# Audio tower layer: second chunk's token chain among the first chunk's projections, norms at other places of the second scan

## The reference

```python
h = patches @ tok_W.T + tok_b                       # 512 features
h = h + block(layernorm(h))                         # mamba and MLP, below
h = h + down(silu(gate(n)) * up(n)),  n = layernorm(h)

# block(x):
zxbcdt = rmsnorm(x, rms1_w) @ in_proj_w.T           # z 1024, x 256, B 256, C 1024, dt 128
dt = softplus(dt_in @ dt_proj_w.T + dt_proj_b)
state = exp(dt * A) * state + (dt * x) * B          # 1024 channels x 16 states, along a token axis
y = (sum over 16 states of C * state + D_skip * x) * silu(z)
h1 = x0 + y @ out_proj_w.T
out = h1 + (silu(hn @ gate_w.T) * (hn @ up_w.T)) @ down_w.T,  hn = rmsnorm(h1, rms2_w)
```

## Time and profile before

| | |
|---|---|
| median of 3 runs | 675.78 us (672.87 to 676.73) |
| the profiled execution: time / span | 675.06 us / 673.3 us |
| busy: PE, PEld, DVE, ACT, POOL | 631.5, 505.7, 418.0, 346.4, 429.2 us |
| mean granted TensorE clock | 0.98 |
| chunk 0's units begin / chunk 1's begin (DVE) | 36.58 us / 204.25 us |
| chunk 0's `out` begins / its first MLP begins (PE) | 218.64 us / 245.81 us |

### The profile page before, as it was taken

The page is one execution under the profiler, slowest core; times in us unless marked ns, Lnnn a source line. Parts: engine busy times, 40 slices in busy tenths (PEclk is TensorE's granted clock), DMA queues, the critical chain, the costliest instruction groups (busy, mean ns, idle before and its releaser), DMA issues.

```text
span 673.3 us, 8617 instructions
## 1 busy us (share of the span) xinstructions
PE 631.5 (94%) x2846; PEld 505.7 (75%) x2846; DVE 418.0 (62%) x532; ACT 346.4 (51%) x773; POOL 429.2 (64%) x244
## 2 busy tenths in 40 slices
PE   4969998799999989999979999999999999999998
PEld 3736765466665757777747777766999998999998
DVE  4077896889887879889887888851322223332132
ACT  4359889358989364434356433422542442653441
POOL 0176785437786999987877987644455463445461
PEclk9879998799999989999989999999999999999999
DMA  8699997489999969988866898533443453134421
GB/s 340 238 365 364 318 299 268 141 258 357 350 373 348 390 250 349 413 336 318 320 247 257 320 330 323 191 125 122 138 149 126 125 157 126 63 130 132 146 67 44
DMA packets 49164, 163.50 MB, mean 243 GB/s; under 512 B 4320, under 2 KB 18528, under 8 KB 48480
## 3 DMA queue, kind: packets, MB, share of 16 engines
q1 hardware_dynamic: 49120, 162.95, 68.9%
HBM read 145.24 MB, written 17.69 MB: 242 GB/s over the span
## 4 chain that ended last, share of the span: by engine, by line
PE 75%; DVE 11%; ACT 5%; POOL 3%; issue 3%; DMA 2%; SPq 0%; DVEq 0%; ACTq 0%; POOLq 0%
PE work L992 54%; PE da L992 15%; DVE da L784 6%; PE work L1002 5%; DVE hs L794 3%; POOL hs L447 2%; ACT L522 2%; ACT da L548 1%; DMA bb<-b_rows 1%; DMA c_rows<-c_rows 1%; DMA sm<-small 0%; POOL hs L460 0%; DVE a L849 0%; ACT z L665 0%; DVE work L809 0%
## 5 line engine op out<-in xcount | busy, mean ns | idle before, releaser
L784 DVE TENSOR_TENSOR_SCAN da<-da,hs 128x580 f32<-128x580 f32 (+1 forms) x128 | 191.1, 1493 | 39.6 <-POOL hs L447 22.2
L447 POOL TENSOR_TENSOR hs<-dtx,bb 128x1160 f32<-128x1160 f32 (+1 forms) x64 | 171.2, 2677 | 61.1 <-PE work L1002 54.1
L426 POOL TENSOR_TENSOR ws<-wraw,ws 128x1024 fp32r<-128x1024 f32 x40 | 101.4, 2536 | 92.8 <-ACT ws L557 92.8
L992 PE MATMUL work<-sq,wraw 128*128 128x290 f32 x512 | 125.7, 406 | 1.1 <-DVE sq L882 1.1
L992 PE MATMUL work<-hn,win 128*128 128x290 f32 (+1 forms) x336 | 104.4, 459 | 16.6 <-DVE hn L857 8.1
L992 PEld LDWEIGHTS work<-sq,wraw 128*128 128x128 f32 x512 | 96.5, 189 | 30.0 <-issue 1.6
L548 ACT ACTIVATE da<-dt,a_neg 128x261 f32<-128x261 f32 (+1 forms) x256 | 118.2, 493 | 0.0
L794 DVE TENSOR_TENSOR hs<-da,cb 128x580 f32<-128x580 f32 (+1 forms) x128 | 105.2, 822 | 10.7 <-DMA cb<-c_rows 2.7
L992 PEld LDWEIGHTS work<-hn,win 128*128 128x128 f32 x336 | 65.5, 200 | 50.7 <-issue 26.0
L545 ACT COPY da<-zeros 128x58 f32<-128x58 f32 (+1 forms) x128 | 27.6, 216 | 126.0 <-DVE hs L794 125.8
L557 ACT CAST ws<-wraw 128x1024 fp32r<-128x1024 f32 x48 | 50.3, 1048 | 70.2 <-PE da L992 34.4
(11 more groups left out here) (98 smaller groups left out, 655.2 us busy)
## 6 DMA issues: line engine op xcount, KB each, us to landing
wraw<-w_stream SPq DMA_DIRECT2D x104, 512.0 KB, 4.1
bb<-b_rows SPq DMA_DIRECT2D x32, 700.0 KB, 7.1
cb<-c_rows SPq DMA_DIRECT2D x32, 700.0 KB, 5.6
bb<-b_rows SPq DMA_DIRECT2D x32, 580.0 KB, 8.0
cb<-c_rows SPq DMA_DIRECT2D x32, 580.0 KB, 6.0
c_rows<-c_rows SPq DMA_DIRECT2D x8, 875.0 KB, 10.8
c_rows<-c_rows SPq DMA_DIRECT2D x8, 725.0 KB, 6.6
win<-w_in SPq DMA_DIRECT2D x4, 1024.0 KB, 13.4
```

The lines of the kernel that those rows point to most:

```text
L426: nc.gpsimd.tensor_tensor(ws[:, k % NW, 1, :], wraw[:, split_loads[k] % NRAW, :], ws[:, k % NW, 0, :].bitcast(F32), ALU.subtract).then_inc ...
L447: nc.gpsimd.tensor_tensor(hs[:, u % NH, 0:NQ * n].rearrange("p (n t) -> p n t", t=n), dtx[:, t % 2, 0:n].unsqueeze(1).to_broadcast([P, NQ, ...
L784: nc.vector.tensor_tensor_scan(da[:, j, 0:w], da[:, j, 0:w], hs[:, u % NH, j * w:(j + 1) * w], 0.0, ALU.mult, ALU.add).then_inc(scan_done, 1)
L992: last = nc.tensor.matmul(dst, w, x, start=(k == 0), stop=(k == len(pairs) - 1))
```

## The change

`tokc` becomes four steps `tok` of one product each, and chunk 1's stand in slots 5, 6, 8 and 9, `mean` in slot 10, `ln1` in 11 and `rms1` in 13, each first in its slot, ahead of chunk 0's projections there. `in_dt`, `in_b` and `in_x` stand in slots 14 to 16, tiles 0 to 5 of chunk 1 in 17 to 28, slot 29 is empty, tile 6's `dtp`, `xs` and `in_z` stand in 30 and 31. Slot 32 is empty. Beside the norms of the second scan stand `in_c` of tile 6 and `in_z` of tile 7 (`rms2`), `dtp` of tile 7 (`ln2_mean`) and `in_c` of tile 7 (`ln2_var`). `tok`, `mean` and `ln1` join `LATE`. Chunk 1's squares go to `th` and `acc`, its reciprocal roots to `rstd` and `rstd_ln`, so that `mean`'s bank is free after L842 and `ln1`'s after L846. ACT does the squares of `rms2` in the slot before it, the root first in its slot, and both for `ln2_var` in the slot of `ln2_mean`. On DVE `PLACE` puts the last two `out` and `rms2` after the first half of their unit, `ln2_mean` after the first scan, `ln2_var` ahead of it. Chunk 0's `gate_y` for tiles 0 to 6 stands in the middle of the unit of quarter 2, not at the end of that of quarter 1.

```diff
+def tokens(c):
+    return [("tok", c, k) for k in range(KD)]
...
-    bg += [[("dtp", 0, 7), ("in_c", 0, 7)], [("xs", 0, 7), ("in_z", 0, 7)]]
-    bg += [[("tokc", 1)], [("mean", 1), ("ln1", 1)], [("rms1", 1)], [("in_dt", 1), ("in_b", 1, 0)],
-           [("in_x", 1, 0), ("in_b", 1, 1)], [("in_x", 1, 1)]]
+    bg += [[("in_c", 0, 7), ("in_z", 0, 7)], [("dtp", 0, 7), ("xs", 0, 7)]]
+
+
+    for u, s in zip((5, 6, 8, 9, 10, 11, 13), tokens(1) + [("mean", 1), ("ln1", 1), ("rms1", 1)]):
+        bg[u].insert(0, s)
+    bg += [[("in_dt", 1), ("in_b", 1, 0)], [("in_x", 1, 0), ("in_b", 1, 1)], [("in_x", 1, 1)]]
     bg += two_tiles(1, 0) + two_tiles(1, 2) + two_tiles(1, 4)
+    bg += [[], [("dtp", 1, 6)], [("xs", 1, 6), ("in_z", 1, 6)]]
     assert len(bg) == UNITS
     slots += list(enumerate(bg))
     o = outs(0)
-    first = [[("dtp", 1, 6), ("in_c", 1, 6), ("xs", 1, 6)], [("xs", 1, 7)], o[0:2], o[2:4]]
+    first = [[], [("xs", 1, 7)], o[0:2], o[2:4]]
     rest, left = [], UNITS - len(first)
     for s in m_steps(0):
 
-        rest += {"rms2": [("in_c", 1, 7), s, ("in_z", 1, 6)], "ln2_mean": [s, ("in_z", 1, 7)],
-                 "ln2_var": [s, ("dtp", 1, 7)]}.get(s[0], [s])
+        rest += {"rms2": [("in_c", 1, 6), s, ("in_z", 1, 7)], "ln2_mean": [s, ("dtp", 1, 7)],
+                 "ln2_var": [s, ("in_c", 1, 7)]}.get(s[0], [s])
...
-LATE = ("dtp", "xs", "in_c", "in_z", "out")
-SEAM = (("in_c", 1, 7), ("in_z", 1, 6), ("in_z", 1, 7), ("dtp", 1, 7))
+LATE = ("dtp", "xs", "in_c", "in_z", "out", "tok", "mean", "ln1")
+SEAM = (("in_c", 1, 6), ("in_z", 1, 7), ("dtp", 1, 7), ("in_c", 1, 7))
+
+PLACE = {("out", 0, 2): 2, ("out", 0, 3): 2, ("rms2", 0): 2, ("ln2_mean", 0): 1, ("ln2_var", 0): 0}
...
-                if kind == "tokc":
-                    if c == 0:
+                if kind == "tok":
+                    k = s[2]
+                    if (c, k) == (0, 0):
                         act.wait_ge(tokb_done, 1)
-                    else:
-                        full(act, ("xs", c - 1, KI - 1))
-                        act.wait_ge(b_stored, 16 * 2 * c)
-                    for k in range(KD):
-                        name = ("tokc", c, k)
-                        full(act, name)
-                        nc.scalar.activation(a(c, k), bank(name), ACT.Identity, bias=tok_bc[:, k:k + 1]).then_inc(centered, 1)
-                        nc.scalar.activation(sq[:, k, 0:n], bank(name), ACT.Square,
-                                             bias=tok_bc[:, k:k + 1]).then_inc(free_of(name), 1)
+                    full(act, s)
+                    nc.scalar.activation(a(c, k), bank(s), ACT.Identity, bias=tok_bc[:, k:k + 1]).then_inc(centered, 1)
+                    nc.scalar.activation(token_square(c, k), bank(s), ACT.Square,
+                                         bias=tok_bc[:, k:k + 1]).then_inc(free_of(s), 1)
...
-                    if v >= 1:
-                        act.wait_ge(norm_done, KD * v)
                     full(act, s)
                     link(nc.scalar.activation(ln, bank(s), ACT.Ln, bias=eps_ap))
                     nc.scalar.activation(inv, ln, ACT.Exp, scale=-1.0).then_inc(inverse_done, 1)
-                    act.wait_ge(h_done, KD * (c + 1))
-                    nc.scalar.activation(bank(("mean", c)), ln, ACT.Exp, scale=-0.5).then_inc(rstd_done, 1)
+                    if c == 0:
+                        act.wait_ge(h_done, KD * (c + 1))
+                        nc.scalar.activation(bank(("mean", c)), ln, ACT.Exp, scale=-0.5).then_inc(rstd_done, 1)
+                    else:
+                        nc.scalar.activation(ln, ln, ACT.Exp, scale=-0.5).then_inc(rstd_done, 1)
...
+                    if c >= 1 and kind == "in_x":
+                        full(act, ("xs", c - 1, KI - 1))
+                    if c >= 1 and kind == "in_b":
+                        act.wait_ge(b_stored, 16 * 2 * c)
+                    if c >= 1 and kind == "in_dt":
+                        full(act, ("dtp", c - 1, KI - 1))
...
-                    norm = [s for s in steps if s[0] in ("rms2", "ln2_var")]
-                    if norm:
-
-                        n = steps.index(norm[0])
-                        between = [steps[n - 1]] if steps[n - 1] == SEAM[2] else []
-                        first = steps[:n - len(between)] + [("squares",) + norm[0]]
-                        second = between + [("root",) + norm[0]] + steps[n + 1:]
+
+                    if i + 1 < len(slots) and ("rms2", 0) in slots[i + 1][1]:
+                        second.insert(0, ("squares", "rms2", 0))
+                    if ("rms2", 0) in steps:
+                        first, second = [("root", "rms2", 0)], [s for s in steps if s[0] != "rms2"]
+                    if ("ln2_mean", 0) in steps:
+                        first = [("squares", "ln2_var", 0), ("root", "ln2_var", 0)]
+                        second = [s for s in steps if s[0] != "ln2_mean"]
+                    if ("ln2_var", 0) in steps:
+                        first, second = [], [s for s in steps if s[0] != "ln2_var"]
...
-                    if unit % QU == 1 and unit > QU:
+
+                    if unit < UNITS and unit % QU == 2 and unit > QU:
+                        parts.insert(2, ("gate", unit // QU - 1))
+                    if unit > UNITS and unit % QU == 1:
                         parts.append(("gate", unit // QU - 1))
...
+                    for s in reversed([s for s in others if s in PLACE]):
+                        parts.insert(PLACE[s], s)
+                    others = [s for s in others if s not in PLACE]
```

More of the change, by code:

```diff
@@ L104, in schedule @@
 def schedule():
-    slots = [(None, [("bmean", 0), ("tokc", 0), ("mean", 0), ("ln1", 0), ("rms1", 0), ("in_dt", 0), ("in_b", 0, 0), ("in_b", 0, 1),
+    slots = [(None, [("bmean", 0), *tokens(0), ("mean", 0), ("ln1", 0), ("rms1", 0), ("in_dt", 0), ("in_b", 0, 0), ("in_b", 0, 1),
                      ("dtp", 0, 0), ("in_c", 0, 0), ("in_x", 0, 0), ("xs", 0, 0)]),
@@ L163, in work_bank_uses @@
                 ring = RINGS[2]
-            names = {"tokc": [("tokc", s[1], k) for k in range(KD)], "rms1": [],
-                     "gu": [(s, "gate"), (s, "up")]}.get(s[0], [s])
+            names = {"rms1": [], "gu": [(s, "gate"), (s, "up")]}.get(s[0], [s])
             for n in names:
@@ L615, in step @@
                     nc.scalar.activation(inv, ln, ACT.Exp, scale=-1.0).then_inc(inverse_done, 1)
[L616 to L617 removed]
+                    if c == 0:
+                        act.wait_ge(h_done, KD * (c + 1))
+                        nc.scalar.activation(bank(("mean", c)), ln, ACT.Exp, scale=-0.5).then_inc(rstd_done, 1)
+                    else:
+                        nc.scalar.activation(ln, ln, ACT.Exp, scale=-0.5).then_inc(rstd_done, 1)
                 elif kind == "rms1":
[L619 removed]
+                    var = bank(("ln1", c)) if c == 0 else rstd[:, 0:n]
                     log_tables()
                     act.wait_ge(scaled_var, c + 1)
[L622 to L623 removed]
+                    link(nc.scalar.activation(rstd[:, 0:n], var, ACT.Ln, bias=eps_ap))
+                    nc.scalar.activation(var, rstd[:, 0:n], ACT.Exp, scale=-0.5).then_inc(rstd_done, 1)
                 elif kind in ("rms2", "ln2_var"):
@@ L706, in step @@
                             gated_high(i)
-            for unit, steps in late(slots, 1):
+            for i, (unit, steps) in enumerate(late(slots, 1)):
                 if unit == 0:
@@ L857, in step @@
                         nc.vector.scalar_tensor_tensor(out=hn[:, k, 0:n], in0=a(c, k), scalar=small_ap(S_W1, k),
-                                                       in1=bank(var), op0=ALU.mult, op1=ALU.mult).then_inc(norm_done, 1)
+                                                       in1=bank(var) if c == 0 else rstd[:, 0:n],
+                                                       op0=ALU.mult, op1=ALU.mult).then_inc(norm_done, 1)
                     dve.wait_ge(norm_done, KD * (v + 1))
-                    dve.sem_inc(free_of(var), 1)
-                    dve.sem_inc(free_of(("mean", c)), 1)
+                    if c == 0:
+                        dve.sem_inc(free_of(var), 1)
+                        dve.sem_inc(free_of(("mean", c)), 1)
                 elif kind == "rms2":
@@ L1041, in step @@
                     product(s, [(mean_w[:, :], sm[:, S_TOKB:S_TOKB + KD])], KD)
-                elif kind == "tokc":
+                elif kind == "tok":
                     pe.wait_ge(pat_loaded, 16 * (c + 1))
                     pe.wait_ge(tokw_done, 1)
-                    for k in range(KD):
-                        product(("tokc", c, k), [(tokw[:, k * P:(k + 1) * P], pat[:, OFF[c]:OFF[c] + n])])
+                    product(s, [(tokw[:, s[2] * P:(s[2] + 1) * P], pat[:, OFF[c]:OFF[c] + n])])
                 elif kind == "mean":
@@ L1049, in step @@
                 elif kind == "ln1":
-                    product(s, [(mean_w[:, :], sq[:, k, 0:n], free_of(("tokc", c, k)), uses[("tokc", c, k)][1] + 1)
```

(1 more changed line is left out.)

20 lines of the change are left out of this document (14 added, 6 removed).

## The result

The changed kernel takes 680.37 us (median of 5 runs, 678.68 to 681.46) against 675.78: 1.0069 times the kernel before, interval 1.0044 to 1.0095. It is slower, where 669 was forecast and faster held most of the chance. Its profiled execution took 678.68 us, with a span of 676.9.

The account below looks back on a forecast made before the run. The prediction took PE, busy 94%, to set the pace, with DVE close behind. It summed +3.0 (scan's end and `out`), -4.5 (`rms2`) and -4.4 (`ln2`) to -5.9 from 675.06, so 669.2, forecast as 669.0; range 658 to 674.

Parts of the forecast that it names:

- the wait for C rows: Near unit 30 of chunk 0's scan: DVE's wait behind six weight loads, 0 to 2.65 us, taken as 1.0.
- PE's gain of 4.0 by ss26: Up to the end of unit 26's state sum on PE: 11.4 us of old losses gone, less 7.4 of new ones.
- what the MLPs give back: Second scan: 2.5 us lost to a bank wait in the MLP behind `ln2`; none counted behind `rms2`.
- the three seams: PE's idle gaps between the chunks, at `rms2` and at `ln2`, with lower clock behind: some 26 us in all.
- The chain among the units: Chunk 0's units: new PE waits of 1.6 (`ln1`), 1.6 (`rms1`), 2.4 and 1.0 us (state sums), plus 0.8 of clock.
- The end of the scan: End of chunk 0's scan: DVE's line of 23.0 us behind ss26 leaves `y_done` of tile 7 unchanged; `out` ends 3.0 later.
- Rival 2: Slots 5 to 11: ACT is overrun, each slot loses a table load's length, 9.0 us more, time 678.2; chance 0.09.
- rival 3: Both MLP starts: DVE, not PE, sets them, half of the norms' 8.9 us returns as bank waits, 673.6; chance 0.15.
- The clock: At `out`: PE's clock falls in 6.5 us of idle time ahead of it, costing 2.0 us (0 to 3.4).
- `rms2`: Chunk 0, end of `out` to first MLP: 6.8 us instead of 11.3, gain 4.5 (0 to 4.5).
- `ln2`: Chunk 0, `ln2_mean` to second MLP: PE starts 6.9 us earlier, 2.5 lost to a bank wait, gain 4.4 (1 to 6.9).
- The gates: Chunk 0's gates in mid-unit: free where PE trails DVE, else state sums wait 2.4 (unit 12) and 1.0 us (unit 16).

Follow-up runs that it names:

- both mended: Changed kernel with the root of the second chunk's first norm kept in PSUM and the six weight loads issued over six slots: 674.40 us, 0.9982.
- The part by itself: Kernel before with only the second scan's steps beside the norms, DVE places and ACT order, tile 6's `in_z` in slot 32: 670.63 us, 0.9922.

## Why the prediction was wrong

**The steps that failed.** The prediction had the chain's move with the end of the scan and `out` at +3.0 us, and expected the norms to outweigh it. In the traces it is +10.0 (from unit 5 to the end of `out`, 186.1 against 176.0). The largest failed term is the wait for C rows, taken as 1.0 and measured as 4.2. The second is PE's gain of 4.0 by ss26, which was 1.6, with an operand's move put at nothing that cost 1.3. The third is what the MLPs give back: nothing and 2.5 were forecast, 1.3 and 4.4 measured.

**What bounds the kernel.** Behind the second term stands a reading that failed too. From PE's 94% and its full windows the prediction took it that PE's gaps between the chunks were PE's to win back. With the chain moved they are not, up to `out(0)`: giving PE 11.9 us of free time instead of 8.1 brought nothing, and DVE's line with its hand-overs to ACT and POOL set the pace. For the kernel before this is argued and not shown, since no run took PE's gaps away and left the chain in place, and DVE waits 6.1 us for PE there. The prediction had half of this, where it said that DVE's pace cannot rise behind ss26. It let DVE's line ahead of ss26 follow PE's, and put PE's 4.0 us of gain into it. On DVE unit 20 came 4.6 us later than before (92.45 us behind unit 5 against 87.84).

**The chain among the units, "PE gains 4.0".** PE gained 9.1 - 7.5 = 1.6 by ss26. Two waits were foreseen well (1.27 for 1.6 at `ln1`, 1.02 for 1.0 at unit 16), but `in_dt` waited 4.05 for 1.6, 1.44 came that was not foreseen, and the lower clock cost 2.2 at `in_dt` (4.60 for 2.36) and not 0.8. That is 10.0 where 7.4 were forecast. Of the miss of 2.4, 1.3 is L876's (139.49 - 138.18): the prediction counted the move of the roots from PSUM to SBUF ("same instructions as before") at nothing. The other 1.3 is still there with both mended (138.37 against 137.05), and `rms1`'s operand may have up to 0.7 of it. The prediction's 26 us for the three seams do not come out of its rows either: 11.4, 2.97 + 1.8 and 4.96 + 1.10 + 1.8 make 24 (1.8 is what a variance at the lower clock takes longer). No later term rests on it.

**The end of the scan.** "DVE has, in line, ... 23.0" was right but for 0.9: 23.94 and 23.93 once the loads don't disturb it. The C-row wait was the mis-sized term, 1.0 in a range of 0 to 2.65, and measured 4.2 (28.1 against 23.9 with the loads spread). The range's upper end came from a row where the wait stands in unit 33. Moved to units 30 and 31, the waits delay the gate behind them and with it unit 28's state sum. The row of before was no price for this: where it stood, spreading the loads gave nothing.

**Rival 2**, slower at 678.2 with `out` beginning after 223, comes near the number (680.37 and 225.65) by chance, since its mechanism is not what happened: seven slots were to lose a table load's length each, and PE waited only twice there, 0.56 and 1.27, the second time for a bank that DVE frees. What did grow is DVE's waiting for ACT between units 5 and 20, from 7.3 to 12.6 us. The rule that the prediction sets beside rival 3 is that of the Trainium skill ("Trainium Kernel Development and Optimization", Best Practices): weight loads' busy share, and not matmul's, tells how near PE is to its limit. The prediction set it aside since the gaps' releasers seemed to speak against the slack. Up to `out(0)` it would have been the better guide, as far as the kernels with the chain moved show. Behind that, 5.9 of the 11.7 us won at the norms came through, in a kernel where the share is 75% all the same.

**The clock** took 2.5 for 2.0 in `out`, inside the stated 0 to 3.4. Not foreseen was a further stretch at the lower clock, 363.8 to 367.2, behind the bank wait of the second MLP.

**`rms2`**: 4.8 for 4.5, right, but the first MLP gave 1.3 back, 1.10 of it in a bank wait for which the prediction had nothing. **`ln2`**: PE begins 6.9 earlier, exactly as worked out, with 0.83 open for the squares (0.8). The bank wait was 2.04 for 2.5; with the smaller ones behind it and the clock, 4.4 are given back in all, so that 2.5 of gain are left and not 4.4. Rival 3 had "half of the 8.9" come back as bank waits; here 5.8 of 11.7 did. The part by itself still gains 0.8% (0.9922).

**The gates** were costed at 3.4 us in two waits. One came, 1.02, and the gates alone gain 0.3%.

What stays open: that DVE's hand-overs with ACT and POOL make unit 20 late, with 2.3 us more idle time than before, was read from the list of waits and is not settled by a run. A version of the chain which spares DVE these waits was not tried, and neither was one with both roots back in PSUM.

## What to carry to other kernels

An idle gap of the busiest engine is a gain only if the next event that all engines wait for comes earlier by closing it. Before moving a chain, follow the line of the engine that the meeting point waits for (here DVE to `y_done`), add the chain's hand-overs to it at the new place, and see if it arrives sooner. Price each change of an operand's place as an instruction of its own, and look up what POOL does beside it at that time. And let each part of a compound change run alone: here a gain of 1.3% was hidden under a loss of 2.0%.

## What the runs showed of the hardware

**A DVE multiply with both operands in SBUF, beside a POOL instruction.** Single ones of L876 took 2.35, 1.11, 1.01 and 1.01 us. With one operand in PSUM they took 0.51 each, although POOL was busy beside most of them too. The timelines of DVE and POOL, first before, then after:

```profile
121.82 1.79 DVE L849 TENSOR_TENSOR a<-a,work 128x350 f32<-128x350 f32 x4
122.27 2.44 POOL L447 TENSOR_TENSOR hs<-dtx,bb 128x1160 f32<-128x1160 f32 x1 [1.88 <-PE work L1002]
```
```profile
101.06 2.45 POOL L461 TENSOR_TENSOR hs<-dtx,bb 128x1160 f32<-128x1160 f32 x1 [6.01 <-PE work L1038]
...
103.48 1.08 POOL L496 TENSOR_TENSOR pair<-sp_w,pair 128x290 f32<-128x290 f32 x1
104.63 0.86 POOL L498 TENSOR_TENSOR pair<-pair 128x290 f32<-128x290 f32 x1
105.57 0.86 POOL L500 TENSOR_TENSOR dt<-dt,pair 128x290 f32<-128x290 f32 x1
```

The first one ends at 103.90, 0.4 behind POOL's 103.51, as if it had run only then; the others alternate with POOL's, which grow too (1.08, 0.86, 0.86 for 0.80, 0.70, 0.70 with the root in PSUM). L885, both operands in SBUF with POOL idle, takes 2.06 for four, and 2.76 in the run where it meets one of POOL. The Trainium skill ("SBUF — State Buffer", SBUF: two separate sides) has this rule: a DVE instruction with two SBUF inputs and a GpSimd instruction that reads SBUF exclude each other for their whole length. The trace agrees, with the 2.35 and the alternation behind it. The prediction overlooked it.

**Queued loads.** Behind six weight loads issued within 2.90 us, C rows on the same queue took 14.87 us from issue to landing, and a later issue took 5.70, where the others there take 0.3 to 1.2. With one load a slot the changed kernel's issues there take 0.32 to 0.69.

**Clock.** Behind 4.99 to 5.99 us of idle time ahead of `out`, its 64 records took 17.68 to 18.67 us; behind 0.45 to 1.34 us, in six other traces, 15.89 or 15.90. The longer ones have a stretch at 1.2 GHz in them (223.8 to 230.7 in the changed kernel).
